# A transformer block on one core: attention and the row projection behind it put into one order of steps

## The chip, the cores and the metric

The kernel runs on one core of a Trainium2 chip. The metric is the device time of one execution in microseconds (us); three executions of the kernel before took 2669.25 us in the median (2667.64 to 2670.5). Engines are named as in the profile: PE is TensorE, DVE VectorE, ACT ScalarE, POOL GpSimd, SP the engine that here only issues transfers.

## The reference

One block on x of 4 x 2048 rows of 256 numbers, in float32. The attention weights come as two factors (down and up), which the kernel folds first.

```
def _L0_attn_ref(x, ...):                 # H = 16 heads, DH = 16
    q = concat([q_c, rope(q_e)]); k = concat([k_c, rope(k_e)])
    scores = einsum('bhqd,bhkd->bhqk', q, k) * DH ** -0.5
    att = softmax(where(causal, scores, -inf))
    y = einsum('bhqk,bhkd->bhqd', att, v)
    return y.transpose(0, 2, 1, 3).reshape(b, t, c) @ Wc
def _L0_ffn_ref(x, ...):                  # 8 experts, 2 per row
    topk_w, topk_idx = top_k(x @ Wr + br, 2); gate = softmax(topk_w) on the two
    h = relu(einsum('th,ehf->etf', x, W1) + b1); y = einsum('etf,efh->eth', h, W2) + b2
    return einsum('te,eth->th', gate, y)
x = x + _L0_attn_ref(_layernorm(x), ...)
x = x + _L0_ffn_ref(_layernorm(x), ...)
```

## The kernel before, in words

The rows are handled in 16 blocks of 512 (NB = 16), four for each of the 4 batches of the input. Four stages follow one another: `project`, `attend`, `mix` and `experts`. The first two are blocks of their own (all engines meet between them and behind them); `mix` and `experts` share one.

**attend** (line 612) walks over 16 groups w, each one batch of the input and four heads. Within a group there are four chunks c of 512 queries, and for each chunk the key tiles kt up to the diagonal: 40 steps a group (STEP_LIST), 640 in all. A step has two parts on PE: *scores* (ps_s, line 932), four pieces of up to 512 columns, handed to ACT in groups of two and one, which takes their exponential (lines 832, 836); and a *sum* (ps_o, line 953), which multiplies the four probabilities with v. POOL zeroes the upper triangle of the first four steps of a chunk (line 802). Ahead of a group's scores its row maxima must be known: *max* pieces (PE line 973, DVE lines 857 and 861), which are worked a group ahead of the sums; their negatives are turned by PE, split by DVE (lines 886, 888) and placed by SP as further rows of q (`place_minus`). When a chunk is summed, ACT copies it out (line 842), PE turns it (line 984), DVE divides (lines 895, 900) and SP stores it into y_dram. The order of all this is one list, PLAN, made by `attention_plan` on the host from costs and hold values; each engine runs through the list and does its own part of each entry. After the last maximum, PLAN has 119 score groups, 46 sums and 5 turn_out entries left. POOL also splits a sixteenth of the expert weights into high and low parts at the end of each group and stores them.

**mix** (line 1001) takes the 16 blocks in turn. For block n, in this order over the engines: turn_y (PE turns the block of y in two halves, line 1439, ACT copies them, line 1179), mix_heads (PE, the product with Wc, 16 matmul records, line 1454), the residual and the statistics (DVE, lines 1315 to 1402), the normalised rows (ACT, line 1187), their turning (PE 1439, ACT 1179), route (PE, line 1466), by_expert (ACT, line 1221), turn_logits (PE, line 1475), the choice of two experts and their weights (DVE), count (PE, lines 1486 and 1490), the place of each row in its expert's list (DVE, lines 1413 to 1424), and eight indirect transfers by POOL that scatter 128 entries each into list_dram (line 1161). In turn n of PE's loop the parts belong to blocks n-2 to n+2: mix_heads(n+1), the turning of block n-1, count(n-2), turn_y(n+2), route(n-1), turn_logits(n-1). list_dram is first filled with a pattern by four transfers of ACT at the head of the stage, and POOL's first scatter waits for them. SP loads y and x four blocks ahead, stores the rows and loads one sixteenth of the split expert weights (1024 KB) per block.

**experts** (line 1577) makes a table of 142 tiles, loads the lists (SP waits until all 128 scatters have landed), gathers rows by POOL and runs both layers on PE.

The line on which POOL waits in `mix`:

```
pool.wait_ge(entries_made, n + 1)
pool.wait_ge(slots_made, n + 1)
```

Of the kernel before, what the change touches and what calls it, by code (L numbers as in the profile page):

```python
# [466 lines left out]
EARLY = 12  # L467
# [5 lines left out]
BUFS = 3  # L473
HOLD = {"max": -171, "scores": -140, "sum": 0, "turn_out": -266}
STEP_LIST = [(w, c, kt) for w in range(NG) for c in range(CH)
# [22 lines left out]
def max_list():  # L498


    turns = [(w, late) for w in range(NG) for late in (False, True)]
    out = []
    for i, (w, late) in enumerate(turns):
        tiles = range(EARLY, QT) if late else range(EARLY)
        pieces = [("max", w, qt, pair, kc) for qt in tiles for pair in range(2) for kc in range(qt // TILES + 1)]
        turn = [("turn_max",) + turns[i - 1]] if i else []
        out += pieces[:AHEAD] + turn + pieces[AHEAD:] + [("chain", w, late)]
    return out + [("turn_max",) + turns[-1]]


def attention_plan(groups, covers):
# [19 lines left out]
    while k < len(groups) or s < len(STEP_LIST) or at < len(maxes) or outs:  # L531
# [8 lines left out]
        if k < len(groups):  # L540
            newest = groups[k][-1][0]
            w, c, _ = STEP_LIST[newest]
            placed = rows.get((w, c == CH - 1))
# [24 lines left out]
        if kind == "max":  # L568
# [3 lines left out]
            if e[0] == "turn_max":  # L572
                tile_free[:] = [start + 60, start + 60]
                vector = max(start + 260, vector - 85) + 543
                rows[e[1:]] = vector + 6500
# [18 lines left out]
        elif kind == "sum":  # L594
# [3 lines left out]
            if STEP_LAST[s]:  # L598
                scalar = copied = max(end + 217, scalar - 108) + 592
                outs.append((s // NSTEP * CH + STEP_LIST[s][1], copied))  # L600
# [11 lines left out]
def attend(nc, parts_dram, v_dram, w1, w2, minus_dram, y_dram, split_dram):  # L612

    GROUPS = score_groups()
    NPIECE = len(STEP_LIST) * GH
    COVERS = [[0] * GH for _ in STEP_LIST]
    for k, g in enumerate(GROUPS):
        for s, h in g:  # L620
            COVERS[s][h] = k
    PLAN = attention_plan(GROUPS, COVERS)
    LOADS = 13


    DIAGS = [0]
    for s, (_, c, kt) in enumerate(STEP_LIST):
        DIAGS.append(DIAGS[-1] + (2 if kt >= c * TILES else 0))

    with ExitStack() as ctx:  # L630
        def sb(name, shape, dt):
            return ctx.enter_context(nc.sbuf_tensor(name, shape, dt))

        def sem(name):
            return ctx.enter_context(nc.semaphore(name))

        q_st = sb("q_st", [P, BUFS, 2, T], F32R)
        k_st = sb("k_st", [P, BUFS, 2, T], F32R)
        v_sb = sb("v_sb", [P, BUFS, QT, GH, VW], F32)
        prob = sb("prob", [P, PROBS * GH, TB], F32)  # L640
        out_sb = sb("out_sb", [P, CH, TB], F32)
        y_sb = sb("y_sb", [P, 2, TILES, GH, DH], F32)
        rec = sb("rec", [P, 2, TILES, GH], F32)
        ident = sb("ident2", [P, P], F32)
        causal = sb("causal", [P, TB], F32)
        junk = sb("junk", [P, SLOTS, 2, TB], F32)
        maxes = sb("maxes", [P, GH, QT, CH], F32)
        minus = sb("minus", [P, GH * EARLY], F32)
        ones = sb("ones", [PARTS, T], F32)
        ffn_raw = sb("ffn_raw", [P, 2, WCH], F32)  # L650
        ffn_hi = sb("ffn_hi", [P, 2, WCH], F32R)
        ffn_lo = sb("ffn_lo", [P, 2, WCH], F32R)
        minus_rows = sb("minus_rows", [GH * EARLY, PARTS, P], F32R)

        ps_s = [ctx.enter_context(nc.psum_tensor(f"ps_s{i}", [P, 2 - i, 512], F32)) for i in range(2)]
        ps_m = [ctx.enter_context(nc.psum_tensor(f"ps_m{i}", [P, 2, 512], F32)) for i in range(SLOTS)]
        ps_o = ctx.enter_context(nc.psum_tensor("ps_o", [P, 512], F32))

        ident_made = sem("ident_made2")
# [334 lines left out]
WORDS = 4  # L994
NT = B * T // P
WLOADS = 4
YB = 4
XB = 4


# [953 lines left out]
```

## Time and profile before

| | us |
|---|---|
| median of three runs | 2669.25 |
| profiled execution, first to last instruction (span) | 2735.5 |
| PE busy in it | 2406.9 (88%) |
| DVE busy | 2048.1 (75%) |
| ACT busy | 1581.1 (58%) |
| POOL busy | 823.7 (30%) |

The profile is of one execution; the page gives no other time of it than the span. A busy time is the sum over an engine's instructions, without waits. For PE the ends of matmuls are modelled. "PEclk" is the granted TensorE clock, 1.00 being 2.4 GHz and 0.50 being 1.2 GHz. "idle before <-releaser" is what ended the idle time ahead of an instruction; "remote" or "another core or an unknown queue" means that the profile found no event that ends it, and on a single core there is no other core.

### The profile page before, as it was taken

The page shows a single profiled execution, that of the slowest core. Times are in us where ns is not written, and L with a number is a line of the kernel's source. Part 1 is how long each engine was busy: PE and PEld are TensorE (multiplying, and loading weights), DVE is VectorE, ACT ScalarE, POOL GpSimd, SP SyncE. Part 2 cuts the span into 40 slices and gives each one's busy share as a digit, 9 for nine tenths or more (in the row PEclk, how much of TensorE's full clock was granted, in tenths as well). Part 3 has the DMA queues.
Part 4 walks back from the last instruction along what each step waited for, and adds up shares of the span by engine and source line. Part 5 has one row for each costly group of instructions (what it writes and reads, how often), then busy time and mean ns, then how long its engine had stood idle before and what let it go on. Part 6 is the DMA issues. An engine that isn't in the chain of part 4 may idle for free. (4 is left out here: it accounts for less than half of the span.)

```text
span 2735.5 us, 48214 instructions
## 1 busy us (share of the span) xinstructions
PE 2406.9 (88%) x15842; PEld 1359.7 (50%) x15842; DVE 2048.1 (75%) x5002; ACT 1581.1 (58%) x2716; POOL 823.7 (30%) x1130
## 2 busy tenths in 40 slices
PE   6885799999999999999999999998777389998998
PEld 6774333333334333333334333332444278887897
DVE  3876989998999898888898998940355457765776
ACT  3663277777777776667777777776433234433443
POOL 1543011211212112111212112121055655555554
PEclk8997699999999999989999999997888689999999
DMA  3777814414504513504414423010675323323332
GB/s 145 261 260 212 113 39 63 74 42 61 86 29 64 86 34 59 84 27 65 83 35 64 80 44 71 8 31 20 236 203 177 94 92 113 107 93 96 111 109 72
DMA packets 147501, 255.95 MB, mean 94 GB/s; under 512 B 72951, under 2 KB 91897, under 8 KB 138916
## 3 DMA queue, kind: packets, MB, share of 16 engines
q1 hardware_dynamic: 114544, 164.96, 27.1%
q0 software_dynamic: 29904, 80.65, 8.9%
q10 hardware_dynamic: 2812, 7.26, 1.5%
q8 instruction: 135, 2.21, 0.3%
q14 instruction: 106, 0.87, 0.1%
HBM read 147.59 MB, written 107.76 MB: 93 GB/s over the span
## 5 line engine op out<-in xcount | busy, mean ns | idle before, releaser
L836 ACT ACTIVATE prob<-ps_s 128x512 f32<-128x512 f32 (+5 forms) x1620 | 1078.1, 714 | 480.5 <-PE ps_s L932 477.8
L857 DVE TENSOR_REDUCE maxes<-ps_m 128x2 f32<-128x1024 f32 x768 | 913.9, 1221 | 107.8 <-PE ps_m L973 104.8
L932 PE MATMUL ps_s<-q_st,k_st 50*128 50x512 f32 (+3 forms) x2560 | 610.2, 413 | 73.8 <-ACT prob L836 57.2
L973 PE MATMUL ps_m<-k_st,q_st 48*128 48x512 f32 (+3 forms) x2560 | 603.2, 443 | 75.9 <-DVE maxes L857 39.6
L953 PE MATMUL ps_o<-prob,v_sb 128*17 128x512 f32 (+3 forms) x5120 | 617.5, 556 | 1.2 <-ACT prob L836 0.7
L802 POOL TENSOR_SCALAR_AFFINE_SELECT prob<-prob 128x256 f32<-128x256 f32 x512 | 203.2, 406 | 1347.8 <-ACT prob L836 1220.8
L973 PEld LDWEIGHTS ps_m<-k_st,q_st 48*128 48x128 f32 x2560 | 272.6, 191 | 531.3 <-DVE maxes L857 256.6
L861 DVE CUSTOM_DVE_ANT_0 junk<-ps_m,causal 128x128 f32<-128x128 f32 (+3 forms) x1024 | 453.1, 484 | 44.2 <-PE ps_m L973 42.7
L932 PEld LDWEIGHTS ps_s<-q_st,k_st 50*128 50x128 f32 x2560 | 318.3, 190 | 306.1 <-ACT prob L836 234.1
L1728 ACT ACTIVATE h_hi<-ps_turned 128x512 fp32r<-128x512 f32 x142 | 85.0, 598 | 225.6 <-PE ps_turned L1843 157.9
L94 PE MATMUL ps_out<-experts_hi,h_lo 128*128 (+1 forms) x568 | 173.0, 305 | 0.0
L953 PEld LDWEIGHTS ps_o<-prob,v_sb 128*17 128x17 f32 x5120 | 86.9, 96 | 171.1 <-issue 141.9
L96 PE MATMUL ps_out<-experts_hi,h_hi 128*128 (+1 forms) x568 | 161.1, 284 | 0.0
L95 PE MATMUL ps_out<-experts_lo,h_hi 128*128 (+1 forms) x568 | 161.0, 283 | 0.0
L1161 POOL DMA_INDIRECT list_dram<-entry,slots x128 | 123.9, 968 | 117.6 <-DVE slots L1424 80.0
L1757 DVE TENSOR_TENSOR h<-ps_hidden,b_sb 128x512 f32<-128x512 f32 x142 | 98.2, 692 | 54.8 <-PE ps_hidden L96 44.9
L1771 DVE TENSOR_TENSOR y<-ps_out,b_sb 128x256 f32<-128x256 f32 x142 | 60.3, 425 | 95.7 <-issue 50.5
L94 PE MATMUL ps_hidden<-experts_hi,x_lo 128*128 (+1 forms) x284 | 127.2, 448 | 1.7 <-DVE x_lo L1752 0.9
L895 DVE RECIPROCAL rec<-ps_m 128x16 f32<-128x16 f32 x64 | 16.2, 254 | 131.2 <-PE ps_m L984 130.3
L96 PE MATMUL ps_hidden<-experts_hi,x_hi 128*128 (+1 forms) x284 | 114.2, 402 | 0.0
L95 PE MATMUL ps_hidden<-experts_lo,x_hi 128*128 (+1 forms) x284 | 114.0, 402 | 0.0
L95 PEld LDWEIGHTS ps_out<-experts_lo,h_hi 128*128 128x128 f32 x568 | 108.8, 191 | 0.1
(187 smaller groups left out, 3180.6 us busy)
## 6 DMA issues: line engine op xcount, KB each, us to landing
parts_dram<-parts SPq DMA_DIRECT2D x64, 512.0 KB, 3.8
q_st<-parts_dram SPq DMA_DIRECT2D x84, 256.0 KB, 8.5
k_st<-parts_dram SPq DMA_DIRECT2D x84, 256.0 KB, 18.4
v_dram<-v_out SPq DMA_DIRECT2D x16, 544.0 KB, 5.5
xin<-in_L_attn_x SPq DMA_DIRECT2D x16, 512.0 KB, 6.0
ffn_raw<-in_L_ffn_W POOLq DMA_DIRECT2D x32, 256.0 KB, 5.2
y_dram<-y_sb SPq DMA_DIRECT2D x64, 128.0 KB, 2.0
split_hi<-ffn_hi POOLq DMA_DIRECT2D x16, 512.0 KB, 3.2
```

Of the source, the lines that this page charges most:

```text
L94: nc.tensor.matmul(out, s_lo, m_hi, start=first, stop=False, skip_group_check=True)
L95: nc.tensor.matmul(out, s_hi, m_lo, start=False, stop=False, skip_group_check=True)
L96: return nc.tensor.matmul(out, s_hi, m_hi, start=False, stop=last, skip_group_check=True)
L802: nc.gpsimd.affine_select(out=tile, in_=tile, compare_op=ALU.is_ge, fill=0.0, base=0, pattern=[[0, 2], [1, P]], channel_multiplier=-1).the ...
L836: last_exp = nc.scalar.activation(prob[:, at:at + n, lo:TB], bank[:, 0:n, lo:TB], ACT.Exp, scale=DH ** -0.5)
L857: return nc.vector.tensor_reduce(maxes[:, 2 * pair:2 * pair + 2, qt, kc], bank[:, :, :], AX.X, ALU.max)
L861: last = nc.vector.tensor_tensor_reduce(junk[:, slot, i, 0:w], bank[:, i, 0:w], causal[:, TB - w:TB], 1.0, NEG, ALU.add, ALU.max, maxes[:, ...
L932: mm = nc.tensor.matmul(ps_s[k % 2][:, i, lo:TB], k_st[half(h % 2, ROWS), w % BUFS, h // 2, kt * P:(kt + 1) * P], q_st[half(h % 2, ROWS), ...
L953: mm = nc.tensor.matmul(ps_o[32 * h:32 * h + VW, lo:TB], v_sb[:, w % BUFS, kt, h, :], prob[:, (s % PROBS) * GH + h, lo:TB], start=STEP_FIR ...
L973: mm = nc.tensor.matmul(ps_m[slot][:, i, 0:wide], q_st[half(i, STACK), w % BUFS, pair, qt * P:(qt + 1) * P], k_st[half(i, STACK), w % BUFS ...
L1161: pool.indirect_dma_start(list_dram[:, :], bass.IndirectOffsetOnAxis(ap=slots[:, j, i:i + 1], axis=0), entry[:, j, i, :], None).then_inc(s ...
L1757: nc.vector.tensor_tensor(out=h[:, s % 2, :], in0=ps_h[s % 2][:, :], in1=b1_sb[:, bass.ds(e, 1), :].rearrange("p a n -> p (a n)"), op=ALU. ...
```

## The change

`attend` and `mix` become one function, `attend_and_mix`, and one block with `experts`. A list of the mix's steps (`mix_steps`) is merged into PLAN (`whole_order`); every engine, SP and POOL too, walks the merged list.

```diff
+YOUT = 4
+YB = 2
+XB = 2
+GATE_LAG = 2
+PLACE_LAG = 3
+EARLY_WEIGHTS = 4
+PE_COST = {"scores": 0.3, "sum": 0.95, "turn_out": 0.6, "turn_y": 0.5, "turn_x": 0.5, "heads": 1.75, "route": 1.75,
+           "logits": 0.45, "count": 0.8}
+def mix_steps():
+    out = [("turn_y", 0, 0), ("turn_y", 0, 1), ("heads", 0, 0), ("heads", 0, 1), ("load_y", 2),
+           ("turn_y", 1, 0), ("turn_y", 1, 1), ("load_y", 3)]
+    for n in range(NB + GATE_LAG):
+        steps = [("vec", n)]
+        if n < NB:
+            steps.append(("store", n))
+        if n + XB < NB:
+            steps.append(("load_x", n + XB))
+        if 1 <= n <= NB:
+            steps += [("xn", n - 1), ("turn_x", n - 1, 0), ("turn_x", n - 1, 1)]
+        if n + 1 < NB:
+            steps += [("heads", n + 1, 0), ("heads", n + 1, 1)]
+        if 1 <= n <= NB:
+            steps.append(("route", n - 1))
+        if n + 2 < NB:
+            steps += [("turn_y", n + 2, 0), ("turn_y", n + 2, 1)]
+        if n + 2 + YB < NB:
+            steps.append(("load_y", n + 2 + YB))
+        if 1 <= n <= NB:
+            steps.append(("logits", n - 1))
+        if n >= GATE_LAG:
+            steps += [("ratio", n - GATE_LAG), ("count", n - GATE_LAG)]
+        scatters = [("scatter", n - PLACE_LAG - 1, i) for i in range(SCATTERS)] if n > PLACE_LAG else []
...
+    out.append(("place", NB - 1))
+    out += [("scatter", NB - 2, i) for i in range(SCATTERS)]
+    out += [("scatter", NB - 1, i) for i in range(SCATTERS)]
+def whole_order(plan):
+    last_turn = max(i for i, e in enumerate(plan) if e[0] == "turn_max")
+    head, tail = list(plan[:last_turn + 1]), list(plan[last_turn + 1:])
...
+    out = head[:at] + first + head[at:] + [("setup",)]
+    steps = mix_steps()
+    held = steps.index(("load_y", NB - CH))
+    inside, behind = steps[:held], steps[held:]
+    share = sum(cost(e) for e in inside) / total
+    for e in tail:
+        out.append(e)
+        done += cost(e)
+        if not early and e[0] == "sum" and e[1] >= (NG - 1) * NSTEP + 2:
+            out += [("weights", k) for k in range(EARLY_WEIGHTS)]
+            early = True
+        while inside and spent < done * share:
+            spent += cost(inside[0])
+            out.append(inside.pop(0))
+    for e in behind:
+        out.append(e)
+        if e[0] == "store":
+            for _ in range(3):
...                                          # three loads of weights per store, until all 16
+    ps_t = [ps_m[0][:, 0, :], ps_s[0][:, 0, :], ps_s[0][:, 1, :]]
+    ps_x = [ps_m[0][:, 1, :], ps_m[1][:, 0, :]]
+    ps_g = ps_m[1][:, 1, :]
+            bank = use % 3 if i > LAST else 0
...
+        def turn_rows(use, rows, a):         # PE: turn_y, turn_x and the last chunks' turn_out
+            bank = BANK[use]
+            if BEFORE[use] is not None:
+                pe.wait_ge(turned_copied, BEFORE[use] + 1)
...
+            elif e[0] == "xn":               # ACT
+                act.wait_ge(scale_made, n + 1)
+            elif e[0] == "load_y":           # SP
+                if n >= YB:
+                    sp.wait_ge(rows_turned, USE["turn_y", n - YB, 1] + 1)
+                sp.wait_ge(y_stored[n % CH], 16 * (n // CH + 1) * HG)
+            elif e[0] == "weights":          # SP
+                if k < EARLY_WEIGHTS:
+                    sp.wait_ge(summed, (NG - 1) * NSTEP)
+                    sp.wait_ge(ffn_out, 32 * NG)
...
+                    sp.wait_ge(summed, len(STEP_LIST))
+            elif e[0] == "scatter":          # POOL
+                if e[2] == 0:
+                    if n == 0:
+                        pool.wait_ge(prefilled, 4 * 16)
+                    pool.wait_ge(entries_made, n + 1)
+                    pool.wait_ge(slots_made, n + 1)
+                if c % 2 and r == TILES - 1 and split < NG:    # POOL, at a sum: twice a group
+                    split_weights(split)
+                    if split == 2:
+                        make_pattern()
+                if number == 3 * CH:         # ACT, behind the copy of the 13th chunk
+                    prefill()
```

In words, what is not seen in these lines. The steps ahead of load_y(12) are *inside*: they are spread between the 170 entries that PLAN has behind the last maximum, in proportion to PE_COST. Counted from the lists, these are 9 of the 18 "vec" turns, 20 of 32 half products with Wc ("heads"), 37 half turnings (21 of y and 16 of x; a 22nd of y falls right behind), 8 route, 7 logits, 6 count and 36 of the 128 scatters; the other 92 scatters are behind. The block of y that a step inside reads belongs to one of the first three batches of the input, which are complete by then. In the attention's last part all turnings use one PSUM bank (bank 0 of ps_t); behind it three. The last five chunks of attention are turned through that bank too and copied back into out_sb by ACT before DVE divides. "logits" are copied to SBUF by ACT and read from there. The constants ahead of `mix` are made at "setup", right behind the last maximum; the mix's weights and the first two blocks of y and x are loaded in group 14. The pattern is put into list_dram after the 13th chunk (group 3). The weights are split in the first eight groups. Buffers of the mix lie where q, k of group 13 and others lay; twelve of the sixteen loads of expert weights wait until attention is done. POOL's identity, and DVE's tables in `experts`, use room that exists already. `project`, the maxima, scores and sums, and the loops of `experts` are the same.

## Rows read from the trace of the kernel before

**Rows 1.** The page: the chain that ended last, by engine.
```profile
PE 22%; another core or an unknown queue 2%; issue 1%; ACT 1%; POOL 1%; DVE 1%; DMA 0%; ACTq 0%; DVEq 0%; SPq 0%; POOLq 0%
```

**Rows 2.** Stretches: us, PE, PEld, DVE, ACT, POOL busy; PEclk, DMA share, GB/s.
```profile
425.00:1800.00 1375.00, 1281.32 (x9100) 534.95 (x9097) 1225.81 (x2675) 996.59 (x1593) 259.62 (x528) 0.98 0.33 58
...
1815.00:1940.00 125.00, 107.21 (x566) 32.21 (x566) 3.86 (x12) 83.67 (x133) 17.49 (x36) 0.79 0.05 14
1940.00:1980.00 40.00, 28.18 (x148) 21.83 (x148) 21.57 (x134) 12.23 (x24) 1.55 (x7) 0.81 0.96 371
1980.00:2185.00 205.00, 130.85 (x720) 79.62 (x718) 112.83 (x690) 67.44 (x136) 123.70 (x128) 0.79 0.55 164
```

**Rows 3.** Timeline, rows that bound the stages: start, us, what [idle before <-releaser].
```profile
1815.20 0.28 DVE L888 TENSOR_TENSOR minus_rows<-ps_m,minus_rows 16x128 fp32r<-16x128 f32 x1
...
1939.09 0.42 DVE L900 TENSOR_TENSOR y_sb<-ps_m,rec 128x256 f32<-128x256 f32 x1
...
1979.78 1.05 POOL L1161 DMA_INDIRECT list_dram<-entry,slots  x1 [36.27 <-DVE slots L1424]
...
2184.03 0.97 POOL L1161 DMA_INDIRECT list_dram<-entry,slots  x1 [0.31 <-issue]
...
2192.52 0.66 PE L1822 MATMUL ps_rows<-ident,xn 128*128 128x128 f32 x2 [28.97 <-ACT xn L1718]
```

**Rows 4.** The page's groups of scores and sums over all 640 steps.
```profile
L932 PE MATMUL ps_s<-q_st,k_st 50*128 50x512 f32 (+3 forms) x2560 | 610.2, 413 | 73.8 <-ACT prob L836 57.2
...
L953 PE MATMUL ps_o<-prob,v_sb 128*17 128x512 f32 (+3 forms) x5120 | 617.5, 556 | 1.2 <-ACT prob L836 0.7
```

**Rows 5.** Timeline of PE, one turn of mix at full clock before any scatter.
```profile
1969.89 1.88 PE L1466 MATMUL ps_r<-xt,wr_sb 128*8 128x512 f32 x4
1972.54 0.41 PE L1475 MATMUL ps_l<-ident,by_expert 8*128 8x8 f32 x4 [0.77 <-ACT by_expert L1221]
1972.88 3.72 PE L1454 MATMUL ps_x<-wc_sb,yt 128*128 128x256 f32 x16
...
1977.31 0.25 PE L1486 MATMUL ps_c<-hot,above_b 128*128 128x16 bf16 x4
1977.42 0.40 PE L1490 MATMUL ps_c<-hot,ones_b 128*128 128x16 bf16 x10
1977.67 1.07 PE L1439 MATMUL ps_turn<-ident,b_sb 128*128 128x128 f32 x8
1978.67 1.88 PE L1466 MATMUL ps_r<-xt,wr_sb 128*8 128x512 f32 x4
```

**Rows 6.** Timeline of PE, a later turn, partly at 1.2 GHz.
```profile
2111.82 2.95 PE L1466 MATMUL ps_r<-xt,wr_sb 128*8 128x512 f32 x4
...
2116.07 5.32 PE L1454 MATMUL ps_x<-wc_sb,yt 128*128 128x256 f32 x16
...
2124.12 1.88 PE L1466 MATMUL ps_r<-xt,wr_sb 128*8 128x512 f32 x4 [0.60 <-ACT xt L1179]
```

**Rows 7.** Timeline, all engines, the last scatters of a batch and what follows.
```profile
2106.67 1.04 PE L1439 MATMUL ps_turn<-ident,xn 128*128 128x128 f32 x8
...
2110.60 1.07 ACT L1179 COPY xt<-ps_turn 128x512 f32<-128x512 f32 x2 [4.75 <-remote]
```

**Rows 8.** Timeline of POOL, firsts and lasts of batches of eight scatters.
```profile
1993.08 0.97 POOL L1161 DMA_INDIRECT list_dram<-entry,slots  x1 [3.32 <-DVE slots L1424]
...
2108.29 0.96 POOL L1161 DMA_INDIRECT list_dram<-entry,slots  x1 [0.30 <-issue]
...
2125.41 0.97 POOL L1161 DMA_INDIRECT list_dram<-entry,slots  x1 [2.95 <-DVE slots L1424]
```

**Rows 9.** Waits from 1942 to 2190 without a releaser: us, times, longest.
```profile
ACT xt L1179 <- remote: 37.5, 10, 5.6
DVE place L1413 <- remote: 26.8, 9, 5.3
```

**Rows 10.** Groups of ACT in mix, by form: count, busy us, mean ns, idle before.
```profile
L1187 ACT ACTIVATE xn<-x,shift,rstd 128x256 f32<-128x256 f32 x64 | 33.0, 585 | 0.0
```

More of the change, by code:

```diff
@@ new lines, with __init__, take @@
+class Room:
+    def __init__(self, buffer, at):
+        self.buffer, self.at = buffer, at
+    def take(self, shape, dt=F32):
+        size = math.prod(shape[1:])
+        words = (size + 1) // 2 if dt is BF16 else size
+        view = self.buffer[0:shape[0], self.at:self.at + words]
+        self.at += words
+        if dt is not F32:
+            view = view.bitcast(dt)
+        names = ["a", "b", "c", "d"][:len(shape) - 1]
+        if len(names) == 1:
+            return view
+        return view.rearrange(f"p ({' '.join(names)}) -> p {' '.join(names)}", **dict(zip(names[1:], shape[2:])))
@@ new lines, in attend_and_mix, with sem @@
+def attend_and_mix(nc, block, top, ident, numbers, run, entry, slots, slots_made, listed, biases_in, experts_in,
+                   parts_dram, v_dram, w1, w2, minus_dram, y_dram, split_dram, x, wc, wr, br, tile_numbers, b1, b2,
+                   rows_dram, pairs_dram, list_dram):
+    GROUPS = score_groups()
+    COVERS = [[0] * GH for _ in STEP_LIST]
+    for k, g in enumerate(GROUPS):
+        for s, h in g:
+            COVERS[s][h] = k
+    PLAN = attention_plan(GROUPS, COVERS)
+    ORDER_OF_ALL = whole_order(PLAN)
+    LOADS = 13
+    DIAGS = [0]
+    for s, (_, c, kt) in enumerate(STEP_LIST):
+        DIAGS.append(DIAGS[-1] + (2 if kt >= c * TILES else 0))
+    def sem(name):
+        return top.enter_context(nc.semaphore(name))
@@ new lines, in attend_and_mix @@
+    best = [small.take([P, TILES]) for _ in range(TOP)]
+    score = small.take([P, TILES, E])
+    rest = small.take([P, TILES, E])
+    best_of = small.take([P, TILES])
+    hot = small.take([P, 2, TILES, TOP, E], BF16)
+    logits_sb = small.take([P, 2, TILES, E])
+    away = small.take([P, TILES])
+    ratio = small.take([P, TILES])
+    share = small.take([P, TILES])
+    whole = small.take([P, TILES])
+    place = small.take([P, TILES, TOP, E])
+    slot = small.take([P, TILES, TOP])
+    ones = Room(spare, 0).take([PARTS, TB])
@@ new lines, in attend_and_mix, with in_order @@
+    held_by = {}
+    for i, e in enumerate(ORDER_OF_ALL):
+        if e[0] in ("turn_y", "turn_x") or e[0] == "turn_out" and e[1] in LATE_OUTS:
+            use = len(BANK)
+            bank = use % 3 if i > LAST else 0
+            USE[e] = use
+            BEFORE.append(held_by.get(bank))
+            held_by[bank] = use
+            BANK.append(bank)
+    def in_order():
+        ring = 0
+        for e in ORDER_OF_ALL:
+            yield e, ring
+            ring += e[0] in ("max", "turn_max") or e[0] == "turn_out" and e[1] not in LATE_OUTS
@@ L1574, in rows_landed, with experts @@
     return 16 * (s // ROWBUFS + 1 + len([t for t in early if t < s and t % ROWBUFS == s % ROWBUFS]))
-def experts(nc, block, slots_made, listed_rows, w_sb, numbers, counts, entry, slots, biases, biases_in, rows_dram, pairs_dram, list_dram, out):
+def experts(nc, block, ident, experts_in, slots_made, listed_rows, w_sb, numbers, counts, entry, slots, biases, biases_in, rows_dram, pairs_dram, list_dram, out):
     w_hi, w_lo = w_sb
```

1580 lines of the change are left out of this document (795 added, 785 removed).

## The prediction

> **What bounds the kernel now.** I read the page's chain first, then the stretches, then the timeline where stages meet. The chain [rows 1] is spread over PE and names 2% of the span, some 55 us, for which no releaser was found. The stretches [rows 2] show why the change sits where it does. Over 1375 us of attention PE is busy 1281 us (93%) at a granted clock of 0.98: nothing can be put between. Behind the last maximum, at 1815 us, DVE has nothing left (3.9 of 125 us), ACT works 84 us, and PE is down as 107 us at a mean clock of 0.79, part of it at 1.2 GHz. There is room. Then comes `mix`, 205 us with scatters, in which no engine is busy for more than 131 us.
>
> The bounds of the stretch are four rows [rows 3]: the last maximum is split at 1815.5, the last chunk is divided at 1939.5, the first scatter starts at 1979.8, the last one ends at 2185.0, and PE's first work in `experts` starts at 2192.5. So: 124.0 us of *tail*, 40.3 us until the first scatter, 205.2 us of scatters, 7.5 us of lists and gathers; 377.0 in all. Nothing before 1815 and behind 2192 is touched by more than small edits.
>
> What sets the pace of the 205 us is the batch of eight scatters. POOL takes 0.96 + 0.30 = 1.26 us for each and then idles for about 3 us on DVE's slots; ten batches take 2125.41 - 1993.08 = 132.3 us, 13.2 us each [rows 8]. PE's own turn is shorter: 8.8 us at full clock before any scatter (1978.67 - 1969.89) [rows 5], and 12.3 us (2124.12 - 2111.82) with a third at 1.2 GHz [rows 6].
>
> **The stall that decides how the result is read.** PE turned a block from 2106.67 to 2107.71, and ACT, which needs nothing else, copied it at 2110.60; between the two POOL started its eighth scatter at 2108.29 and ended it at 2109.25 [rows 7, 8]. Such waits sum to 37.5 us on ACT, and most of DVE's 26.8 us stand beside them [rows 9]. The profiled execution spans 2735.5 us and the median run takes 2669.25: 66 us less, although a run's time holds its span. These waits are the only thing in the trace of that size. I take it that they are longer in the profiled execution than in a measured run, so I work out both.
>
> **The tail with the mix's steps in it.** PE's scores and sums cost (610.2 + 617.5) / 640 = 1.92 us a step [rows 4], with 46 steps 88 us. The 37 half turnings cost 0.535 us, 19.8; the 20 half products 1.86, 37.2; eight route 1.88, 15.0; seven logits 0.41, 2.9; six counts 0.65, 3.9 [rows 5]. That is 78.8 us of mix and 167 us of PE work at 2.4 GHz.
>
> To it come the waits of a list that every engine walks in order. xn(n) stands straight ahead of turn_x(n): PE reaches the turning, ACT must first end its last exponential and then write xn, 33.0 / 16 = 2.06 us [rows 10], with nothing for PE between. With one bank, each turning waits for ACT's copy of the one before, some 0.5 us each (1.07 for two in [rows 7]); where scores stand between it is free, and about one pair per block has none. I put 3.5 us on each of eight blocks, 28 us: 195 us in all.
>
> The bounds: at 93% busy the 167 us take 180 us, and 170 if some work overlaps more than the page's means say. From above: the tail as it is and 8.6 turns of 12.3 us in series [rows 6] are 124 + 106 = 230 us. I keep 170 and 230 and take 195, nearer to the lower one, since PE's loop at full clock had only 0.8 us of waiting a turn [rows 5].
>
> The other engines have room in 195 us: ACT 84 + 8 x 2.06 + 42 copies at 0.54 = 123 us and under 10 of small work; DVE 9 turns of (112.8 + 21.6) / 16 = 8.4 us [rows 2]; POOL 17.5 + 36 x 1.26 = 63 us. POOL's scatters stand singly between its masks, so a mask is late by at most 1.3 us, unless POOL waits for slots; place(n) is three turns behind and the scatter a fourth, so the slots are there. The queue behind such a wait would be masks, and PE's sums behind them.
>
> **Behind the tail.** 92 scatters are left, 11.5 batches. At the pace of the trace they take 11.5 x 13.2 = 152 us; without any waiting 92 x 1.26 = 116 us. With the first, from 1815: 195 + 152 + 7.5 = 354.5 us instead of 377.0, 22.5 us less. In a run without the stalls both sides shrink: before, 128 x 1.26 = 161 instead of 205 us (44 less); after, 116 instead of 152 (36 less); the gain is then 22.5 - 8 = 14.5 us. The stalls cancel nearly, as long as they do to the new order what they did to the old one. In the first reading 40.3 us of start are gone (the meeting of the engines, first loads, constants, two turns without a scatter, the lists' pattern), with 36 scatters at 1.65 us, 59 us, against 71 us more of tail and 6 us by which sixteen batches at 13.2 exceed the 205.2 that they took.
>
> **What else moves.** SP loads 4 of 16 MB of weights in the tail, where the DMA engines are 5% busy [rows 2], and 12 MB in four turns behind it, with 1.5 MB of rows a turn: 18 MB, at the 371 GB/s of the stretch from 1940 to 1980 [rows 2] 49 us, against 4 x 13.2 = 53 us. It is hidden by the scatters; if turns were 10 us it would cost up to 9. The next block's y and x stand behind 3 MB (8 us) in SP's queue and are needed two turns later. SP's wait for the whole attention stands ahead of the fifth load of weights, which is behind the last sum in the list anyway. The pattern's four transfers cost ACT some 3 us of issue in group 3, where it is busy 72% [rows 2]; between 0 and 3 us, I take 0. Splitting weights twice a group has the same instructions; POOL is busy 19% there, and they come behind a chunk's last mask: 0, at most 2 us. Copying five chunks back costs ACT 3 us in the tail, and no engine waits. `experts` keeps its loops; its identity (0.5 us) was beside a transfer of lists.
>
> The profiled frame and the median's agree within 8 us, so I take 21 us off the median, nearer to the trace's own difference: **2648 us**.
>
> **The rivals.**
> *The clock (slower).* Place: the tail. PE's granted clock was 0.79 in the mean both in the tail and in `mix`, where PE waited for ACT every few us, and 0.98 in attention, where maxima filled its gaps [rows 2]. The new tail has filled gaps and new waits, and either level could hold. A product with Wc then takes 5.32 instead of 3.72 us, a route 2.95 and more instead of 1.88 [rows 6]. At a mean of 0.79 the 167 us become 211, with 28 of waits 239 us, 44 more than forecast: 2648 + 44 = 2692 us. It decides from a tail of 195 + 21 = 216 us. Against it: ACT has more to do as well, so PE's waits come in shorter pieces than before.
> The Trainium skill (Perfetto Trace Analysis, "Per-instruction lifecycle", on the Tensor engine) says that a matmul's end in a profile is worked out from its size and not observed. By that PE may be at work through what looks like the stall of [rows 7]; a turn would then cost PE up to 12.3 us in the tail as well, 230 us, and the time would be 2683, on the same side. The trace speaks against it as far as the turn before the first scatter goes, 8.8 us with every release in place. Its chance is within that of the clock.
> *The stalls are real and go away.* If measured runs have them in full and single scatters between other work cause none, then 205 us are saved from and 116 are paid: 195 + 116 + 7.5 = 318.5, 58.5 us less, 2611 us. For it: in the trace they come only late in a row of eight scatters. Against it: the 66 us, and POOL goes through its 92 scatters in rows of eight or longer.
> The Trainium skill (Runtime: NRT & Kernel Launch, "The ~15µs preamble/postamble breakdown") says that a profile's total exceeds the time reported for the execution by some 6.2 us whatever the kernel. By that 60 of the 66 us are unexplained; it leaves this rival more chance than I would give it from the rows alone. No row here splits the 66 us.
> *Nothing is won.* Every wait in the tail is exposed, with ACT's exponentials starved after each: 5 us more on each of four blocks, or the two small edits at their upper ends: 2669 us. In effect the work was moved without being overlapped.
>
> **How the numbers follow.** Forecast 0.44 (2625 to 2664), the clock 0.26, stalls gone 0.17, nothing won 0.13. 0.2% is 5.3 us and about what a measurement tells from no change. Faster by more: 0.42 of the forecast and 0.17, 0.59. Within: 0.02 and 0.12 of "nothing won", 0.14. Slower: 0.26 and 0.01, 0.27. The likeliest case's own range is 2625 to 2664. The whole range goes from 2602, below "stalls gone", to 2692, the clock's price; the tail of 170 us (25 less, 2623) and of 230 us (35 more, 2683) are in it.
>
> **What would show it.** Right: a distance of about 195 us from the last minus_rows to the last division; PE busy over 80% of it at a clock above 0.9; some 36 scatters before its end, and 116 to 152 us of scatters behind; PE's first work in `experts` 20 us nearer to the last maximum than 377. The waits of PE for xn should be near 3 us and number eight. Wrong: a clock below 0.85 in that stretch, a stretch above 216 us, masks waited for by sums, or POOL idle behind the tail on anything but slots.

## The result

| | median us | lowest to highest |
|---|---|---|
| before | 2669.9 | 2667.6 to 2677.7 (4 runs) |
| after | 2722.3 | 2710.6 to 2728.1 (4 runs) |
| ratio | 1.018 | 95% interval 1.013 to 1.023 |

The change makes the kernel 1.8% slower; forecast were 2648 us and a range that ends at 2692. The profiled execution of the changed kernel took 2710.64 us and spans 2708.4: 27 us *less* than the first profile of the kernel before, 2735.5. The two profiles can't be subtracted. So the first experiment is a second profile of the kernel before, and most of what follows is read against that one. Some executions of every kernel come out over 1.5% longer than its fastest one; the ratios leave these out.

### The profile page after: what moved, and what is told of

It reads as the page before. It is cut to its first block, busy times and chain, and to the rows that moved or that the text cites. A ratio compares the mean times of both kernels' runs of the same rounds, so it can differ in the third digit from the quotient of the medians.

```text
span 2708.4 us, 48332 instructions
## 1 busy us (share of the span) xinstructions
PE 2398.3 (89%) x15842; PEld 1359.5 (50%) x15842; DVE 2038.8 (75%) x5002; ACT 1585.9 (59%) x2737; POOL 823.6 (30%) x1129
## 4 chain that ended last, share of the span: by engine, by line
PE 69%; DVE 8%; ACT 7%; issue 3%; DMA 2%; POOL 1%; ACTq 1%; SPq 0%; DVEq 0%; POOLq 0%
PE ps_o L1574 19%; PE ps_s L1553 14%; PE ps_m L1591 12%; DVE maxes L1229 6%; ACT prob L1158 5%; PE ps_hidden L94 3%; PE ps_out L94 3%; PE ps_out L96 3%; PE ps_out L95 3%; PE ps_hidden L95 2%; PE ps_hidden L96 2%; PE ps_m L1631 2%; PE ps_turned L2004 2%; DVE junk L1233 2%; PE ps_rows L1983 1%
## 5 line engine op out<-in xcount | busy, mean ns | idle before, releaser
L94 PEld LDWEIGHTS ps_out<-experts_hi,h_lo 128*128 128x128 f32 x568 | 106.8, 188 | 0.5 <-issue 0.4
```

The costliest lines, as they stand in the source:

```text
L94: nc.tensor.matmul(out, s_lo, m_hi, start=first, stop=False, skip_group_check=True)
```

## The profile after

The bounds of the stages, as in [rows 3] (start, duration, engine, line):

```profile
1822.89 0.28 DVE L1480 TENSOR_TENSOR minus_rows<-ps_m,minus_rows 16x128 fp32r<-16x128 f32 x1
...
1919.23 1.04 POOL L1108 DMA_INDIRECT list_dram<-entry,slots  x1 [0.35 <-issue]
...
2049.78 0.42 DVE L1498 TENSOR_TENSOR y_sb<-out_sb,rec 128x256 f32<-128x256 f32 x1
...
2177.67 0.97 POOL L1108 DMA_INDIRECT list_dram<-entry,slots  x1 [0.30 <-issue]
...
2187.02 0.66 PE L1983 MATMUL ps_rows<-ident,xn 128*128 128x128 f32 x2 [33.97 <-ACT xn L1879]
```

The tail is 227.0 us long (1823.2 to 2050.2; forecast 195), 128.4 us follow until the last scatter ends, 8.4 until `experts` begins: 363.8 in all.

The same two stretches (columns as in [rows 2]):

```profile
1823.20:2050.20 227.00, 189.48 (x1026) 91.42 (x1026) 63.33 (x407) 128.37 (x227) 59.31 (x80) 0.86 0.28 87
2050.20:2178.60 128.40, 71.80 (x408) 46.53 (x408) 66.30 (x425) 37.91 (x86) 77.31 (x80) 0.73 0.64 191
```

POOL's 80 instructions in the first stretch are 48 scatters and 32 masks; PE is busy 189.5 us, more than the 167 that the prediction worked out for full clock, and idle for 37.5.

What was waited for in the tail (engine, tile, line, releaser: us, times, longest):

```profile
POOL prob L1092 <- ACT prob L1158: 133.0, 16, 42.2
DVE rec L1493 <- ACT out_sb L1139: 82.2, 5, 20.8
ACT prob L1158 <- PE ps_s L1553: 57.8, 39, 5.0
DVE small L1314 <- ACT small L1213: 44.1, 5, 11.2
...
PEld ps_m L1530 <- ACT big L1184: 23.7, 8, 3.8
...
PE ps_m L1530 <- ACT big L1184: 16.9, 8, 3.4
PE ps_m L1530 <- ACT big L1139: 10.1, 16, 1.1
```

L1184 is xn. PEld is PE's weight load: its row for xn and PE's show the same eight waits, at the load (3.0 us each) and at the matmul behind it (2.1 us each). They must not be added to 40.6 us in 16 waits, as the expectations below do; all of PE's idle time is 37.5 us. "Idle" of POOL and DVE is large and harmless. What costs are the last three rows, because they stop PE. Now the timeline at one block, all engines:

```profile
1940.93 0.73 PE L1553 MATMUL ps_s<-q_st,k_st 50*128 50x512 f32 x3
...
1944.14 0.66 PE L1530 MATMUL ps_m<-ident,big 128*128 128x128 f32 x4
...
1948.55 0.17 DVE L1314 TENSOR_SCALAR small<-small 128x4 f32<-128x4 f32 x1 [11.16 <-ACT small L1213]
...
1950.03 2.06 ACT L1184 ACTIVATE big<-big,small 128x256 f32<-128x256 f32 x4
...
1952.15 1.11 PE L1530 MATMUL ps_m<-ident,big 128*128 128x128 f32 x4 [2.71 <-ACT big L1184]
...
1953.19 1.22 PE L1553 MATMUL ps_s<-q_st,k_st 50*128 50x512 f32 x3
```

PE waits 2.71 us for xn; the half turning then takes 1.11 us, where the one at 1944.14 took 0.66, and three scores take 1.22 instead of 0.73. Behind the wait PE runs at the lower level of 1.2 GHz (granted clock 1.00 from 1945 to 1949 us, 0.50 from 1952.1 to 1954.4); the mean from 1915 to 1960 us is 0.81.

Behind the tail (2050 to 2187):

```profile
POOL list_dram L1108 <- DVE slots L1345: 36.6, 7, 17.8
...
DVE big L1355 <- DMA big<-in_L_attn_x: 25.7, 3, 13.7
```

POOL waits for slots, and DVE for the blocks of x that SP loads behind three loads of expert weights. There are no waits "<- remote" anywhere in this profile.

And one place that I had not looked for, in group 3. ACT, then the stretch from 640 to 660 us:

```profile
635.54 0.67 ACTq L1127 DMA_DIRECT2D list_dram<-spare  x1
...
637.69 6.85 ACTq L1135 DMA_DIRECT2D pairs_dram<-spare  x1
644.64 1.19 ACT L1158 ACTIVATE prob<-ps_s 128x768 f32<-128x768 f32 x2 [7.96 <-issue]
```

```profile
640.00:660.00 20.00, 14.38 (x71) 6.32 (x71) 7.98 (x25) 8.05 (x15) 8.40 (x12) 0.57 1.02 235
```

The fourth transfer of the prefill sat 6.85 us in ACT's queue, and the exponentials behind it. PE was busy 14.4 of 20 us, and its clock fell to 0.57 in the mean.

## Experiments

A ratio is to the kernel before, run in turns on the same chip. The kernels of one part ran together. Medians of the kernel before on the five chips: 2675, 2736, 2677, 2744 and 2668 us. On the second and fourth, the slow chips, the profiles have waits "<- remote", called unexplained below (last section).

### First part: the kernel before again, and one edit each

**The kernel before, profiled again.**

> The kernel before, profiled once more; nothing is changed. Its first profiled execution took 2737.7 us against a median of 2669.9. My theory: that execution was out of the ordinary as a whole, and the 2669.9 us are real work done without the waits that had no releaser; then a second profile spans 2665 to 2680 us, the last maximum is split at 1800 to 1810 us, from there to the first expert matmul it is about 335 us (377 before), and the experts take some 520 us (543 before). By this the change made the stretch between them some 28 us longer (363.8 us in its own profile). The rival, on which the prediction rested: such waits belong to every profiled execution; then this one spans 2725 to 2745 us and again shows 25 to 40 us of ACT's and DVE's waits without a releaser between the tail and the lists.

2658.5 us, span 2656.8, and not one wait "<- remote": what the prediction had assumed fell. My theory had the direction, but three of its four numbers were missed: the span is below 2665, the last maximum is split at 1818.1 and not by 1810, and the stretch takes 320 us and not 335. The experts' 519 us came as expected. Tail, and from there to the last scatter's end:

```profile
1818.10:1923.20 105.10, 88.17 (x566) 28.99 (x566) 3.40 (x10) 82.99 (x132) 17.50 (x36) 1.00 0.05 16
1923.20:2130.10 206.90, 137.60 (x866) 96.15 (x866) 132.72 (x824) 79.84 (x160) 125.22 (x135) 0.83 0.75 235
```

The 88 us of attention's PE work stand in 105.1 us at full clock, not in 124.0 at 0.79 as in the first profile ([rows 2]). Neither tail has a wait "<- remote", and over 105 us of each the weight loads of the scores wait about alike for the exponentials (49.4 us in 55 waits then, 46.7 in 67 now). So the waits alone don't set the clock; why the first profile had the lower level in its tail stays open. The first scatter starts at 1964.65 and the last ends at 2130.1: 165.5 us for 128, 1.29 each, POOL's own pace. In all 319.6 us instead of 377.0 [rows 3]. The changed kernel takes 44.2 us more in this stretch, 5.1 more before it and 2.3 behind: 51.6, the whole difference of the two spans, and near the measured one (52.4). Both profiled executions are 11 to 12 us shorter than their medians.

**Nothing between the sums.**

```diff
-    held = steps.index(("load_y", NB - CH))
+    held = 0
```

> The changed kernel with nothing between the last group's sums: all of the mix's steps stand behind the last chunk's division; buffers, banks, early lists and all else as changed. If the interleaving itself loses (waits for xn, ACT's order, the clock in the tail), this is faster than the changed kernel, 2680 to 2700 us. If it pays and the rest of the change costs (lists prefilled in group 3, three turning banks shared, two buffers instead of four), this is slower than the changed kernel's 2722: a tail of about 125 us and then sixteen batches of 10 to 13 us, 2735 to 2750 us.

1.0071 (1.0031 to 1.0111): of the 1.8%, about 1.1 is the interleaving and 0.7 the rest of the change, each uncertain by some 0.6, as the two were not measured side by side. The profile:

```profile
1817.00:1923.40 106.40, 90.00 (x576) 30.43 (x576) 5.28 (x47) 85.90 (x138) 12.77 (x32) 1.00 0.12 46
1923.40:2145.40 222.00, 146.44 (x857) 99.52 (x856) 124.68 (x788) 78.75 (x175) 124.32 (x128) 0.85 0.57 177
```

Against 227.0 and 128.4 us, the nine turns inside lengthen the tail by 120.6 and save 93.6. Against the kernel before the tail is alike, and the loss stands behind it, 222.0 us instead of 206.9.

**Lists prefilled by SP.**

```diff
-                if number == 3 * CH:          # ACT
-                    prefill()
+            elif e[0] == "sum" and e[1] == 3 * NSTEP + TILES - 1:    # SP
+                sp.wait_ge(summed, e[1] + 1)
+                prefill()
```

> The changed kernel with the four transfers that prefill the lists issued by SP at the same chunk instead of ACT. In the profile of the changed kernel the fourth held ACT's queue for 6.85 us, PE waited, its granted clock was 0.57 from 640 to 660 us, and the maxima of that group were split some 12 us later than before. If it is the issue on ACT that costs, this gives back 10 to 15 us: 2707 to 2712. If it is the transfer's traffic (DMA share 1.02 in those 20 us) that delays the loads, or if the loss of that stretch is regained later, it stays within 4 us of 2722.

1.0108 (1.0060 to 1.0156). From 640 to 660 us:

```profile
640.00:660.00 20.00, 19.27 (x142) 8.37 (x140) 18.25 (x57) 15.29 (x27) 9.47 (x15) 1.00 1.02 162
```

The DMA share is the same 1.02, the clock is 1.00, and from the previous split of maxima to this one it is 38.6 us (612.00 to 650.60) instead of 50.3 (607.86 to 658.15): 11.7 back. It was the place in ACT's queue, not the traffic. On SP's queue the second transfer sat 19.26 us and the new maxima behind it were stored 11 us late, without loss: the next split follows 56.3 us later, as in the kernel before. The Trainium skill (PSUM — Partial Sum Buffer, "Engine vs sequencer instructions") says that ACT's queue is strictly first in, first out; the 7.96 us before the next exponential agree.

That is the gain in group 3. How much of it reaches the time is not shown. This profile is level with that of the changed kernel at the last maximum (1822.1 against 1823.2), because in between its clock fell once with PE at work all the time:

```profile
870.00:885.00 15.00, 14.95 (x63) 5.38 (x55) 7.68 (x18) 7.29 (x10) 0.00 (x0) 0.50 0.00 0
```

Such falls move the last maximum by more than the prefill does. Over the ten profiles of changed kernels without waits "<- remote" it is split at 1817 us in the mean with SP's prefill (six, 1806 to 1831) and at 1826 with ACT's (four, 1817 to 1837). The ratio points the same way, but its interval meets that of the changed kernel (1.013 to 1.023), and at 2699 us the median is lower than the 2707 to 2712 that I expected.

**xn turned behind the next products.**

```diff
-            steps += [("xn", n - 1), ("turn_x", n - 1, 0), ("turn_x", n - 1, 1)]
+            steps.append(("xn", n - 1))
         if n + 1 < NB:
             steps += [("heads", n + 1, 0), ("heads", n + 1, 1)]
+        if 1 <= n <= NB:
+            steps += [("turn_x", n - 1, 0), ("turn_x", n - 1, 1)]
```

> The changed kernel with the turning of xn placed behind the next block's products with Wc, so that PE has 3.7 us of work while ACT writes xn. In the tail of the changed kernel PE and its weight loads wait 40.6 us for xn (16 times, the longest 3.8 us), eight blocks. If these waits set the tail's length (227 us instead of the forecast 195), 15 to 30 us go: 2692 to 2707. If ACT's own order is the bound (its exponentials wait for scores that stand behind), the wait only moves to route's or the exponentials' place: within 5 us of 2722.

1.0061 (1.0022 to 1.0099), 0.012 below the change, with intervals that don't meet, though not measured side by side. The tail:

```profile
1837.00:2043.40 206.40, 180.56 (x1026) 86.45 (x1027) 62.53 (x409) 127.22 (x227) 59.59 (x80) 0.92 0.31 96
```

20.6 us shorter, with no wait of PE for xn left among its rows, and the clock up from 0.86 to 0.92 with no other edit: PE's busy time for the same instructions falls from 189.5 to 180.6. Here the clock came back with the waits gone, and this is more than the scatter of profiles: the three with turn_x directly behind xn on chips without unexplained waits (the change, lists by SP, norm first) have tails of 227.0, 228.2 and 226.6 us, all at 0.86.

### Second part: the change itself, and the repairs together

> The changed kernel itself, again, as the measure for the three that run beside it on this chip: 1.013 to 1.023 of the kernel before, some 2715 to 2725 us.

1.0108 (1.0059 to 1.0157), lower than I expected; the interval meets that of the first measurement. This is the first of the two slow chips; its ratios are compared with each other only.

**Weights two at a time, behind x.**

```diff
-        if e[0] == "store":
-            for _ in range(3):
+        if e[0] == "load_x" or e[0] == "store" and e[1] + XB >= NB:
+            for _ in range(2):
```

> The changed kernel with the twelve late loads of expert weights issued two at a time behind a turn's load of x instead of three ahead of it. Behind the tail of the changed kernel DVE waited 25.7 us for x in three waits, the longest 13.7, with the DMA share at 0.99 for 50 us. If these waits set the 128 us behind the tail, 10 to 20 us go: a ratio 0.004 to 0.008 below the changed kernel's. If the last blocks' way through PE, ACT and DVE is the limit whatever the loads do, the ratio stays within 0.002.

1.0103 (1.0048 to 1.0158): no effect, but the test decides nothing, since its cause was absent on this chip. The changed kernel's own profile there has DVE wait 1.5 us for x, once, and the edited one's has no such wait, against 25.7 us in the profile that the edit was made for. On the chips without unexplained waits DVE waits 18.8 to 27.3 us for x in the four other kernels with three loads ahead, and none to 12.4 in the five with this edit. What that is worth in time shows only together with other edits.

**All three repairs, interleaved; and with nothing inside.**

> The changed kernel with all three repairs: lists prefilled by SP, the turning of xn behind the next products with Wc, and the weights as above. If the causes add, their gains do: 10 for the prefill, 22 for xn, 10 for the weights, 2675 to 2685 us, about the kernel before. If the loss lies in the interleaving as such (PE's work of the mix is in series with attention's, while in the kernel before POOL's scatters hid it), it stays over 1.005 of the kernel before, whatever is repaired.

> The same three repairs, with nothing between the last group's sums. Without repairs that form stood at 1.007, with 16 us more from the first to the last scatter than in the kernel before, 54 us of PE's waits for xn and 27 of DVE's for x. If these waits are what it lost, this equals the kernel before (0.998 to 1.002) or beats it by the first scatter's earlier start; if the three turning banks and two loading buffers cost of themselves, it stays at 1.004 or more. Against the form with everything inside: if interleaving is a loss by itself, this is the faster of the two by 5 to 20 us; if its loss was the waits, the other one is at least as fast.

1.0032 (1.0000 to 1.0064) and 0.9997 (0.9957 to 1.0036). Beside the changed kernel on the same chip (1.0108) the three repairs give back 0.0076, 21 us, clear of noise and half of the 42 that adding them up had promised. The form without interleaving is back at the kernel before; the other is nearly there and no better.

### Third part: what else holds the tail

**Norm first.** In DVE's turn the block's norm is put ahead of the gate and the places of earlier blocks (abridged):

```diff
-            if normal: residual(n)
-            if placing: share_of(d)           # waits for ACT's ratio
-            if normal: (bn_stats ... shift, a step of the gate between each two)
+            if n < NB: residual(n), bn_stats ... shift
+            if placing: share_of(d) ...
+            if gating: gate_best(0, logits) ...
```

> The changed kernel with one edit: DVE's turn first takes the residual and the whole norm of block n, and only then the entries, places and gate of the blocks before. In the profile of the changed kernel DVE stood 11.16 us at 1948.55 for ACT's ratio, the last step of the turn before, which stands in ACT's queue behind exponentials; the norm of the next block stood behind that wait, xn behind the norm, and PE waited 3.02 us for xn. If this chain makes PE's waits in the tail, PE's 40.6 us for xn go down to under 15 and the ratio falls by 0.006 to 0.010 from the changed kernel's 1.011 to 1.018. If ACT's lateness alone makes them, the waits for xn stay above 30 us and the ratio within 0.003.

1.0179 (1.0142 to 1.0216). My chain from ratio to PE fell. DVE's own wait shrank, and PE's did not move by a tenth:

```profile
PEld ps_m L1499 <- ACT big L1184: 23.7, 8, 3.8
...
DVE small L1314 <- ACT small L1213: 20.8, 4, 6.6
PE ps_m L1499 <- ACT big L1184: 16.9, 8, 3.4
```

Norm was ready in time. The wait is ACT's turn: end an exponential, write xn (2.06 us), nothing for PE between.

**Four repairs; a lag of one turn more; nothing inside.** The second has `GATE_LAG = 3`, `PLACE_LAG = 4` and ratio in mid-turn instead of the norm first.

> The three repairs (lists by SP, turning of xn behind the products, weights behind x) and the norm first, interleaved as in the change. With the three the ratio was 1.003. If the waits for xn were the rest of the loss, the tail falls below 195 us with PE's clock above 0.95 in it, and the ratio to 0.993 to 0.999. If the interleaving is a zero-sum (what the tail grows by is what the scatters behind it no longer hide), it stays at 1.001 to 1.005.

> The three repairs, with the gate one turn later (a lag of 3 and 4 turns instead of 2 and 3) and ratio in the middle of the turn instead of at its end; DVE keeps its interleaved order. It takes away the same wait as the norm first, without making DVE's turn longer, but costs one more turn, some 8 us, before the first scatter and none of POOL's work. If DVE's wait for the turn before is the cause, the tail is below 195 us here too, and the ratio 0.995 to 1.001. If it is not, the ratio is above 1.004.

> The same four repairs as in the second of these, with nothing between the last group's sums; with three of them the ratio was 0.9997. Behind the tail ACT has no exponentials and DVE's wait is short, so the norm first should do little: 0.996 to 1.001. It is the measure for what the interleaving itself gives: by the forecast's own sum the interleaved form should beat it by 15 us or more; by the zero-sum theory the two are within 0.003.

0.9997 (0.9966 to 1.0028), 0.9995 (0.9966 to 1.0024) and 0.9992 (0.9953 to 1.0032). Three orders, one time. Tails of 202.3, 199.2 and 107.8 us, then 115.0, 121.9 and 208.7 to the last scatter. Against nothing inside, nine turns inside add 94.5 to the tail and take away 93.7: the zero-sum, for this order. My mark of "below 195" was missed in both, and the first ratio lies between the ranges of my two theories.

### Fourth part: one part alone, few turns inside, and PE's last waits

**The kernel before with its lists prefilled early, by SP, and nothing else of the change.** It was measured on two chips, first on one and then on another.

> The kernel before with one part of the change alone: the lists are prefilled in group 3, by SP, and not at the start of mix. In the second profile of the kernel before, ACT issued those four transfers for 13.5 us before its first copy of a turned y, with the DMA share at 0.96, and POOL's first scatter came 41 us behind the last division. If the prefill delays the first scatter, 8 to 13 us go: ratio 0.995 to 0.997. If the first loads and the weights hold the DMA engines in those 40 us anyway, the ratio is within 0.002 of 1.

> The kernel before with the early prefill by SP alone, again, since 0.9965 with an interval of 0.992 to 1.001 leaves open whether it gains. In its first profile the first scatter came 39.6 us behind the last division, against 40.3 and 41.4 in the two profiles of the kernel before. If that profile is the rule, the prefill hid behind the first loads and the ratio is 0.999 to 1.001; if ACT's 13.5 us of issue held the first turns, it is again 0.995 to 0.998.

0.9965 (0.9924 to 1.0007), then 1.0006 (0.9969 to 1.0043). In the second profile the first scatter comes 38.6 us behind the last division instead of 41.4. Both intervals hold 1: no gain shown. With the prefill gone, ACT's first copy of y comes 7.9 us behind the last division instead of 12.0, and what it waits for now is PE's turning of y.

**Three turns inside.** `held = steps.index(("load_y", 6))` in the kernel of the next paragraph.

> The interleaved form with all repairs and with each pair of half turnings parted by other work of PE, but only the first three turns between the sums (no scatter stands there), the rest behind. The zero-sum theory: a turn costs the tail about 11 us and saves 10 to 12 behind it wherever it stands, so the ratio is within 0.003 of the next kernel's. If PE's idle time in the tail (17 of 105 us in the kernel before) can be filled for free by a little work, this has the best of both: a tail of 125 to 130 us, first scatter within 10 us of its end, ratio 0.993 to 0.997.

1.0023 (0.9984 to 1.0061). The first scatter comes 8.8 us behind the tail as expected (1966.1 against 1957.3), but the tail is 136.2 us: 28 more than the 107.8 with nothing inside, for 27 us more of PE's busy time (118.3 against 91.3). PE's idle time was not filled. This chip was one with the unexplained waits; none of them stands in this tail.

**Half turnings parted.** Order in a turn: xn, heads 0, turn_x 0, heads 1, turn_x 1, turn_y 0, route, turn_y 1. Measured on two chips; the last of the three has DVE's turn as in the change.

> All four repairs, nine turns inside, and each pair of half turnings parted by a half product or the route, so that PE does not wait for ACT's copy out of the one bank (10.9 us in 19 waits in the tail of the form with four repairs). If PE's waits are what the tail has over its 167 us of work, it falls from 202 to some 190 us and the ratio from 0.9997 to 0.995 to 0.997. If ACT's copies then only come later and the exponentials with them, the tail stays at 200 or more and the ratio within 0.002 of 1.

> The interleaved form with all repairs and parted half turnings, again: its profile was one with 116 us of ACT's and DVE's waits that have no releaser. In a profile without them I expect a tail of 190 to 198 us (202 with the pairs together) and the ratio 0.996 to 1.000. If PE's waits for the one bank were hidden elsewhere, the tail is 200 to 205 us.

> The same with DVE's turn as in the change (norm and gate of two blocks interleaved) instead of the norm first. The norm first adds some 15 us to DVE's work in the tail (78 instead of 63) and behind it (83 instead of 66), where POOL waits for DVE's slots. If DVE's order matters for what follows the turning of xn, this is 5 to 10 us slower than the one before it; if not, the two are within 0.002.

1.0002 (0.9968 to 1.0037) on a chip with the unexplained waits, where the tail was 225.1 us instead of the 190 that I expected; 0.9944 (0.9909 to 0.9978) and 0.9981 (0.9946 to 1.0016) on one without. The tail of the second:

```profile
1830.50:2025.00 194.50, 172.57 (x1025) 83.35 (x1025) 77.66 (x411) 126.47 (x227) 59.37 (x80) 0.96 0.33 101
2025.00:2138.30 113.30, 64.73 (x409) 41.07 (x408) 83.49 (x425) 38.83 (x86) 77.43 (x80) 0.76 0.73 216
```

PE's waits for ACT's copies out of the one bank are down from 10.9 us to 6.4, the clock is 0.96, and the tail is 194.5 us. The third has 194.0 and 112.9: the order on DVE makes no difference that can be told. Whether this form beats the kernel before in general is not settled: one of three measurements excludes 1.

## Why the prediction was wrong

Its sum without stalls was 195 + 116 + 7.5 = 318.5 us behind the last maximum against 332.8 before. Measured: 363.8 against 319.6. The step that failed is the first term: 167 us of PE work at 2.4 GHz and 28 us of waits side by side, 195 us of tail; it measured 227.0. From 2648 to 2722.3 are 74 us: 32 for the tail, 13 for the base, 12 for what stands behind the tail, 1 for the lists, 7 outside the stretch, 7 by which the 21 taken exceed the 14.5 that this sum gave, and 1 to 2 of difference between medians and spans. Step by step:

**The tail (the step that failed first).** Forecast 167 us of work and 28 of waits. There were 189.5 and 37.5: 32 us more, two thirds of it in busy time. The number of waits for xn was right, eight, 3.0 us each at the weight load; their price was not. I had seen the order, turn_x straight behind xn "with nothing for PE between", and put 3.5 us on each block. I added the waits to the work at full clock and kept the clock as a rival of 0.26, when in this order the one came with the other: the profiles with fewer waits have a higher clock in the tail, 0.86, 0.92, 0.94, 0.96, and tails of 227.0, 206.4, 202.3 and 194.5 us. It is shown for this kernel's tail and is no rule: my reading of [rows 2], where I put the 0.79 of the tail down to waits for ACT, fell with the second profile, which has near the same waits at 1.00. The clock rival named the right place and the right side, and its mark of 216 us was passed; its price (0.79, 239 us) was too high, and 2692 us too low for what else was missed. The last form's 194.5 us are the forecast's 195 to half a microsecond, partly by luck: they are 172.6 of work and 21.9 of idle time, in an order that the change did not have.

**Behind the tail.** 128.4 us lie within 116 to 152, by luck: POOL had done 48 scatters by the last division, not 36, since nothing in the list makes its scatters wait for that division. For the 80 left its pace gives 103 us, so 25 were waits, for slots behind late x and xn. SP's loads, which I held hidden, or worth "up to 9", stood ahead of x: 25.7 us of DVE's waits. In the last form 113 us are left.

**The base.** The tail of 124.0 us and the waits that are "longer in the profiled execution than in a measured run" were read from one profile. The second shows a tail of 105.1. My reasoning from the 66 us was right in part: executions as short as the median have none of these waits. But they are not made by profiling: on a slow chip the changed kernel's profiled execution, with 98 us of them, took the median's time (2760.6 and 2760.7 us). And more differed than the scatters: the tail by 19 us, the scatters by 40, the experts by 24. In the form without stalls my 161 us for 128 scatters agree with 165.5. By the true base even the forecast's own 318.5 us would have gained 1 us, not 14.5. That is why the repaired kernels, which come near that sum (325.3 us, then 316.2), stop near 1.000.

**The prefill.** "Between 0 and 3 us, I take 0" was 11.7 in group 3: I priced the issue by count and not by what stands in ACT's queue behind it. What it costs the whole kernel is open; at the last maximum the changed kernel is 5.1 us behind the kernel before.

**The rivals.** "The stalls are real and go away" did not come about: the changed kernel has 98 us of such waits on a slow chip as well, and the kernel before none in its second profile. "Nothing is won" named the right end for the form with the repairs. The 6.2 us that the Trainium skill (Runtime: NRT & Kernel Launch, "The ~15µs preamble/postamble breakdown") gives are the excess of a profile's total, which is not the span used here: the time exceeds the span, by 2.2 us in the profile of the changed kernel and 1.7 in that of the kernel before. No run tests the figure, and it had no bearing on the 66 us. Of the rule on modelled ends (the Trainium skill, Perfetto Trace Analysis, "Per-instruction lifecycle") no run shows anything new.

## What to carry to other kernels

Before work is moved into an engine's idle time, take a second profile of the kernel before, and work out both sides on an execution whose time equals the median. Work that was hidden behind a slower engine (PE's behind POOL's scatters) is not free where it goes: the best form's tail is 87 us longer than with nothing inside (81 of them PE's busy time), and what follows it 95 us shorter; the two profiles are from different chips, and no run has that form's order with nothing inside. In one order for all engines, put other work of the consumer between a producer's step and its use, and never a run of transfers in the queue of an engine that feeds PE.

## What the runs showed of the hardware

On two of the five chips the kernels took some 2.5% longer (the kernel before 2736 and 2744 us instead of 2668 to 2677), and all seven profiles from these, of seven kernels, have ACT's and DVE's waits without a releaser; on the other three chips none of the eleven profiles has one. The changed kernel and the form with the three repairs and nothing inside on such a chip:

```profile
ACT big L1139 <- remote: 37.3, 9, 7.2
DVE big L1355 <- remote: 12.1, 2, 7.3
ACT x_hi L1885 <- remote: 12.0, 3, 4.7
```

```profile
ACT big L1144 <- remote: 48.3, 8, 7.4
ACT x_hi L1888 <- remote: 11.1, 3, 4.5
```

All of them sum to 98 and 87 us over the two spans and stand above all in `mix` and `experts`. The median of the kernel before is 60 to 76 us higher on such a chip, that of the changed kernel 38 (2760.7 against 2722.3); so a ratio from one kind of chip can't be set against one from the other. The first profile of the kernel before was such an execution (101 us), beside three runs of 2667.6 to 2670.5 us, the time of chips whose profiles have none. What these waits are stays open.

The granted clock can also be at its lower level for 15 us while PE is busy all the time (0.50 from 870 to 885 us in the profile with the lists prefilled by SP, 14.95 us busy), and the same tail ran at 0.79 in one profile of the kernel before and at 1.00 in the next (0.80 and 1.00 in the two profiles of that kernel with early lists). A difference of 10 us between two single profiles of attention shows nothing.
